# Products of the identity matrix in eleven waits of TensorE, and two GpSimd memsets moved behind a later signal

## What is computed

```python
x = _layernorm(x + _L0_attn_ref(x, ...))         # gated selective scan (state 16), then a GELU feed-forward
x = _layernorm(x + _L0_xattn_ref(x, ctx, ...))   # 16 heads of 64 over ctx, rotary keys
x = _layernorm(x + _L0_ffn_ref(x, ...))          # 8 experts, each 128 -> 512 -> 128, top 2 by a router
x = _layernorm(x + _L1_attn_ref(x, ...))         # latent attention, 16 heads of 8, rotary
x = _layernorm(x + _L1_xattn_ref(x, ctx, ctx, mask, ...))  # 16 heads of 8 over ctx, masked
x = _layernorm(x + _L1_ffn_ref(x, ...))          # 32 experts of 64, top 6 by groups, and a shared expert
```

## Time and profile before

| | |
|---|---|
| median of 3 runs | 538.3 us (536.81 to 538.79) |
| the profiled execution's own time | 538.49 us |
| its span, first to last instruction | 536.7 us |
| mean granted clock of TensorE | 0.891 |
| TensorE busy | 426.9 us (80%) |
| VectorE, ScalarE, GpSimd busy | 317.9, 205.1, 141.0 us |

### The profile page before, as it was taken

The page is one execution under the profiler, slowest core; times in us unless marked ns, Lnnn a source line. Parts: engine busy times, 40 slices in busy tenths (PEclk is TensorE's granted clock), DMA queues, the critical chain, the costliest instruction groups (busy, mean ns, idle before and its releaser), DMA issues.

```text
span 536.7 us, 6915 instructions
## 1 busy us (share of the span) xinstructions
PE 426.9 (80%) x2568; PEld 247.9 (46%) x2576; DVE 317.9 (59%) x741; ACT 205.1 (38%) x257; POOL 141.0 (26%) x133
## 2 busy tenths in 40 slices
PE   0628957489999999869999558697377989967994
PEld 0306624244444445546777425444133444544484
DVE  4579944627766765551511477863696776225754
ACT  0555613142333233114333348764133445622800
POOL 3205733337777665430000300000100000001500
PEclk9967977889999999978999875999687999985998
DMA  8511000000004111150051250000000000000000
GB/s 317 196 28 42 2 0 1 1 2 0 1 0 158 40 39 40 37 204 2 33 94 26 40 64 5 3 4 1 0 1 2 2 1 3 1 31 0 1 0 21
DMA packets 7358, 19.36 MB, mean 36 GB/s; under 512 B 1750, under 2 KB 3126, under 8 KB 6806
## 3 DMA queue, kind: packets, MB, share of 16 engines
q1 hardware_dynamic: 7324, 18.91, 12.0%
HBM read 17.26 MB, written 1.15 MB: 34 GB/s over the span
## 4 chain that ended last, share of the span: by engine, by line
PE 42%; DVE 26%; POOL 15%; issue 12%; ACT 3%; DMA 1%; POOLq 0%; another core or an unknown queue 0%; DVEq 0%
PE ps L1190 39%; POOL big L540 7%; DVE ps L1043 4%; POOL big L547 4%; POOL rstd L490 2%; DVE mx_a L1047 2%; DVE stats L773 2%; DVE big L866 2%; DVE ps L861 2%; POOL big L522 1%; DVE normed L783 1%; PE ps L1197 1%; DVE x L783 1%; DVE meanvar L776 1%; PE ps L1553 1%
## 5 line engine op out<-in xcount | busy, mean ns | idle before, releaser
L1190 PE MATMUL ps<-big,late 128*32 128x256 f32 (+4 forms) x792 | 103.3, 386 | 13.8 <-DVE mx_x L1043 4.0
L1190 PE MATMUL ps<-late,big 128*128 128x128 f32 (+1 forms) x448 | 64.8, 277 | 3.8 <-DVE mx_x L1043 2.2
L1190 PEld LDWEIGHTS ps<-big,late 128*32 128x32 f32 (+3 forms) x800 | 39.7, 117 | 55.3 <-issue 26.8
L726 ACT ACTIVATE big<-ps 128x1024 f32<-128x1024 f32 x48 | 49.0, 1023 | 39.9 <-PE ps L1190 39.6
L488 POOL TENSOR_SCALAR vareps<-meanvar 128x4 f32<-128x4 f32 (+1 forms) x11 | 2.5, 229 | 224.9 <-DVE meanvar L776 224.9
L1190 PEld LDWEIGHTS ps<-late,big 128*128 128x128 f32 (+1 forms) x448 | 45.0, 152 | 27.3 <-issue 20.6
L664 ACT ACTIVATE big<-ps 128x1024 f32<-128x1024 f32 x32 | 32.8, 1024 | 64.8 <-PE ps L1190 52.9
L540 POOL TENSOR_TENSOR big<-big 128x512 f32<-128x512 f32 x32 | 40.5, 1267 | 43.3 <-DVE big L926 43.3
L1043 DVE CUSTOM_DVE_ANT_0 ps<-ps,big 128x512 f32<-128x512 f32 x64 | 42.6, 717 | 12.2 <-PE ps L1190 9.0
L926 DVE TENSOR_SCALAR big<-big 128x1024 f32<-128x1024 f32 x32 | 25.4, 793 | 39.8 <-ACT big L664 39.8
L1190 PE MATMUL ps<-big 64*128 64x256 f32 (+1 forms) x320 | 47.4, 410 | 1.7 <-POOL big L547 1.0
(11 more groups left out here) (229 smaller groups left out, 655.4 us busy)
## 6 DMA issues: line engine op xcount, KB each, us to landing
attn_w<-in_w_x SPq DMA_DIRECT2D x1, 2560.0 KB, 13.2
big<-parts_kx SPq DMA_DIRECT2D x18, 128.0 KB
late<-in_w_up SPq DMA_DIRECT2D x1, 2048.0 KB, 7.8
late<-in_w_dn SPq DMA_DIRECT2D x4, 512.0 KB, 3.8
attn_w<-in_w_up SPq DMA_DIRECT2D x1, 1024.0 KB, 7.9
attn_w<-in_w_dn SPq DMA_DIRECT2D x1, 1024.0 KB, 10.3
parts_kx<-ctx_r SPq DMA_DIRECT2D x1, 768.0 KB, 3.2
rowv<-in_rowv SPq DMA_DIRECT2D x1, 576.0 KB, 4.3
```

The lines of the kernel that those rows point to most:

```text
L726: nc.scalar.activation(ex1[:, n % 3, :].rearrange("p (r n) -> p r n", r=2), ps[:, 2 * (n % 2):2 * (n % 2) + 2, :], ACT.Exp, scale=scale).t ...
L1190: return nc.tensor.matmul(o, lhsT, rhs, start=start, stop=stop, skip_group_check=shared)
```

## The change

`idle_work(bank, n)` multiplies the identity matrix by itself n times (128 x 128 by 128 x 128, float32) into columns 0 to 127 of a PSUM bank that nobody reads before it is written anew. It waits for nothing and signals nothing. It is called at eleven places of TensorE's program with n from 4 to 14, 106 products in all. In GpSimd's program the wait for `y0_ps` (end of sublayer 2) is gone, and both memsets stand behind a wait for `x_k_parts`.

```diff
             root("post1")
+            pool.wait_ge(S["x_k_parts"], PARTS)
             link(nc.gpsimd.memset(sel1, -FAR))
-            pool.wait_ge(S["y0_ps"], 1)
             nc.gpsimd.memset(half_x[1], 0.0).then_inc(S["x_zero1"], 1)
...
+            def idle_work(bank, n):
+
+                for _ in range(n):
+                    mm(ps[:, bank, 0:P], ident[:], ident[:])
...
+            idle_work(5, 8)
             y_of(3)
+            idle_work(5, 4)
             pe.wait_ge(S["yv_done"], 1)
             to_rows(5, [cv[:, 1, :]], [w_mix[:, 5, :]], "mo_ps")
             for i in range(2):
                 keys0(0, 0, i)
+            idle_work(1, 6)
             to_cols(0, normed, "xT_ps", "ln2")
...
+            idle_work(2, 10)
             to_cols(0, normed, "xT_ps", "lat")
...
+            idle_work(1, 10)
             to_cols(0, x, "xT_ps", "post1")
...
+            idle_work(1, 14)
             to_cols(0, x, "xT_ps", "post2")
...
                 total = B * 4 * nk
 
+                idle_work(4 if L == "a" else 6, 10)
                 for n in spreads_after(-1):
                     spread(n)
+                    if L == "a" and n == 0:
+                        idle_work(7, 10)
...
+            idle_work(1, 12)
             to_cols(0, x, "xT_ps", "post3")
...
+            idle_work(1, 12)
             to_cols(0, x, "xT_ps", "post4")
```

## The result

The changed kernel takes 533.08 us (median of 5 runs, 532.03 to 534.63) against 538.3 us for the kernel before beside it (536.81 to 539.19). The ratio is 0.9908, 95% interval 0.988 to 0.9936: faster by 0.9%, 5.2 us.

A forecast was written before the change was run, and what follows sets the result against it. It took TensorE work on the path behind wait gaps, paid at half clock, as the cost to cut; terms 1.7 + 0 + 2.6 + 0.9 + 2.5 + 1.4 + 0.8 = 9.9 us gave a median of 528.4, range 522 to 534.

The forecast's parts named there:

- The likeliest case: Whole kernel: some gaps bridged and some not, 526 to 531 us, chance 0.49.
- the first rival: Norm gaps: the clock still drops at every one, so only 1.7 + 2.6 + 2.5 remain, 531.5 us; chance 0.25.
- The fast rival: Whole kernel: the clock holds everywhere, ln2 and lat too, 17.8 us gained, 520.5 us; chance 0.15.
- Scan end: y_of(3) and the mo products at the scan's end: both waits bridged, clock holds, 1.7 us gained.
- ln2 and lat: Gaps before the feed-forward and at lat: the clock drops anyway, only later; 0 us, ends -0.9 and +4.
- post1: Norm gap before the experts' router: moved memsets free VectorE (1.45 us), clock gives 1.15; 2.6 us, ends 0.5 and 4.
- The memsets' new place: GpSimd memsets beside the sum of expert 2: may hold it up 2.0 us, VectorE idle behind it; cost 0.
- post2: Norm gap before the next projection: 2.0 us if the clock held, taken as open, so half: 0.9 us (0 to 2.0).
- attend a: Attention stage a: two groups of ten products speed its first queries and rows at full clock; 2.5 us (1 to 4).
- post3 and attend x: Norm gap and attention stage x: clock held gives 2.2 us, two in three, so 1.4 us (0 to 2.3).
- post4: Norm gap before the last routing chain: transposes and gate products faster; 0.8 us (-2.2 to 1.4).
- The mean clock: Whole kernel: sign to look for, mean granted clock up from 0.891 to about 0.94.

The follow-up runs named there:

- experiment 9: The kernel before with only the products at the scan's end (8 and 4); 537.8 us, ratio to before 0.9962.
- Experiment 3: The changed kernel without the products at ln2 (6), lat (10) and post2 (14); 530.28 us, ratio to before 0.9851.
- Experiment 6: The changed kernel with more products ahead of, between and behind the transposes at ln2 and lat; 527.43 us, ratio to before 0.9786.
- experiment 1: The kernel before with only the two GpSimd memsets moved later, no identity products; 534.8 us, ratio to before 0.9919.
- experiment 5: The changed kernel without the ten products at post1; 529.97 us, ratio to before 0.9828.
- experiment 7: The changed kernel without products at ln2, lat, post2 and post1, with 12 before the last sublayer's cmb_done wait; 530.07 us, ratio to before 0.9835.
- experiment 10: The changed kernel with all waits filled: ln2, lat, norm gaps, attention 0's last output, attend a, cmb wait; none ahead at post1; 522.29 us, ratio to before 0.9674.
- the repeat: The changed kernel run again unaltered, beside the kernel before; 532.55 us, ratio to before 0.9866.
- experiment 8: The changed kernel with attend a filled through: 14 products ahead of the first query spread, 3 ahead of the next eight; 530.11 us, ratio to before 0.9843.
- experiment 2: The changed kernel with the memsets back in their old place, all 106 products kept; 532.45 us, ratio to before 0.9888.
- Experiment 4: The changed kernel with 12 more products before TensorE's wait for cmb_done in the last sublayer; 532.65 us, ratio to before 0.9863.

## Why the prediction was right, and where it was off

The direction and the range held (533.08 in 522 to 534), 0.9 us from the range's slow edge; the gain was 5.2 us, about half of the 9.9 forecast. The likeliest case alone (526 to 531) missed, and the time lies nearer to the 531.5 of the first rival, in which the clock drops at every norm gap. That rival is not what happened either: the clock held behind post3 and post4. (The fast rival's 520.5 is added up from smaller upper ends than the steps state, 3, 3.5 and 1.3 for 4, 4 and 1.4; by the stated ones it would be 518.9.) By the prediction's own steps:

- *Scan end, 1.7.* Measured 1.7, and shown alone by experiment 9.
- *ln2 and lat, 0.* Measured -0.1 us, with the clock at 0.50 behind both, as said. Experiment 3 takes the groups out and loses nothing. Experiment 6 shows that the clock can be held there and is then worth 2.5 us, inside the 4 given as upper end.
- *post1, 2.6.* Measured 2.8, and the mechanism is shown: the memset held VectorE up (experiment 1, 3.4 us against 3.3). One part of the step was wrong. I credited 1.15 us to a clock that the products hold, and from the router to the second group of up-projections 1.1 us did come; but experiments 1, 5 and 7 gain 0.9 to 1.1 there without products, and experiment 5 has 1.7 us more in all. The products there were a pure cost, as their 2.4 us "stick out" had half said.
- *The memsets' new place, 0.* It stands, but not because VectorE could afford the delay: there was none, 1.13 us beside a running memset. The Trainium skill, "SBUF — State Buffer" (Who interferes with whom), says that tensor_scalar can contend with GpSimd and that an instruction with at most one SBUF input, outside the two-port modes, doesn't. The trace agrees: the L783 rows fell to 1.25 us once the memset was away, and the L969 sum, whose other large input comes from PSUM, kept its 1.13.
- *post2, 0.9.* Measured 0.2. This step took half of "clock held"; the clock was low in both executions of the changed kernel, from 302.2 on in the first, just as the projections began. With the same fourteen products it held in experiments 5 and 6 and gave 1.8 us, near the upper end of 2.0, as in experiment 10 with three more behind the transposes. So "open, half" was a fair statement, and 0.2 was the worse of two outcomes.
- *attend a, 2.5.* **The step that failed.** Measured 0.2, -0.5 in the repeat, and 0.9 with the clock at 1.00 for the whole stage (experiment 8). I took it that the two groups keep the clock up for most of the stage's first 17 us and that what this gives is kept. In its place stands this: behind the two groups the clock falls somewhere in the stage, from 319.2 to 329.5 in one execution, from 319.8 to 323.2 and from 340.3 to 347.1 in the other, at 339.1 in experiment 3. Up to there a held clock is worth 1.9 us (experiments 2 and 3), inside the forecast 1 to 4. A low stretch around 340 then takes 1.0 us (experiments 2 and 3) to 2.4 (the repeat) of it back, because VectorE, which had come early, waits for TensorE. Holding the clock by more products, as experiment 8 does, costs about 1 of the 1.9.
- *post3 and attend x, 1.4.* Measured 1.8; experiments 2, 3, 6 and 8 had 2.9, over the upper end of 2.3.
- *post4, 0.8.* Its own reach gave 0.8: the cmb transposes were 6.9 ahead at y of x and 7.7 when they began. But behind them the term turned to -0.9. **This step looked no further than the routing chain.** It did not ask where TensorE would wait next if it came earlier: at the cmb wait, 3.28 us instead of 0.50, where the clock fell and the up-projections went from 5.32 to 7.01 us. Experiment 4 fills that wait and gets the 1.7 us back in its trace.

The two misses make 2.3 + 1.7 = 4.0 of the 3.9 us between the forecast sum of 9.9 and the 6.0 of the profiled executions; post2's 0.7 is balanced by post1, attend x and the start-up. The rest of the way, from 6.0 to 5.2, is the spread of single executions.

The mean clock was forecast well (0.94, measured 0.936) and says little. Of 49 us of slow time taken away 6 came back as time; in experiment 10 2 x (1 - 0.958) x 520.4 = 44 us stay slow, and 16 came back. I had expected attend a at full clock for most of its first 17 us, and in the changed kernel it was at half for 10 of them.

What stays open: what decides where in attend a the low stretch falls, and what decides whether fourteen products hold the clock at post2. Nothing in the traces tells it; in attend a, two executions with the same instructions differ. Therefore a stage's gain from one pair of profiles is good to about 1 to 2 us, and only scan end, post1, the last sublayer and ln2 with lat are each backed by an experiment of their own. The 1.9 us for attend a are an estimate from its first part, and post3 and post4 were never tried alone.

## What to carry to other kernels

Filler work for the clock is sure to pay only when it bridges a wait, the pieces between and behind the transposes included (at ln2 and lat products ahead alone gave nothing, filled through 2.5 us), and when real work that bounds the stage stands right behind; put it never in front of work whose data are ready (ten products there cost 1.7 us). When TensorE gets faster, look for the next place where it now waits and fill that too: half the job gave 0.9% (1.3% when run again), nearly the whole of it 3.3%. Look also for long GpSimd memsets beside VectorE's SBUF work on the path: moving two of them gave 3.4 us with no other change.

## What the runs showed of the hardware that I had not expected

- Transposes of the identity hold TensorE's clock as products do: 1.00 from 45.9 to 223.2 us, ratio 0.9792 against 0.9786.
- A 3.51 us memset on GpSimd stretches four VectorE normalising operations (SBUF in and out) from 1.25 to 4.44 us, and leaves four sums with a PSUM input at 1.13.
- The same fourteen products ahead of post2's transposes left the clock at 0.50 behind them in five profiled executions (the projection took 4.51 us in the changed kernel's) and at 1.00 in two (experiments 5 and 6, 2.81 us).
- In which part of attend a the clock falls differs between executions of the same instructions: from 319.3 to 329.4 us in one, at 340.4 to 347.0 in another.
